# Keeping the relu result and the mean in PSUM in a graph-convolution kernel

## What is computed

```python
def _sage_conv(x, src, dst, W_l, b_l, W_r):
    agg = jax.ops.segment_sum(x[src], dst, num_segments=N_NODES)
    deg = jax.ops.segment_sum(ones(E), dst, num_segments=N_NODES)
    mean = agg / jnp.maximum(deg, 1.0)[:, None]
    return mean @ W_l + b_l + x @ W_r

h = relu(_sage_conv(x, src, dst, W1_l, b1, W1_r))
h = relu(_sage_conv(h, src, dst, W2_l, b2, W2_r))
return _layernorm(x + h @ W3 + b3)
```

## Time and profile before

| what | value |
|---|---|
| timed runs, median of 3 | 2997.61 us (2995.03 to 3005.15) |
| span of the profiled execution | 2989.1 us |
| PE busy | 2869.4 us, 96% |
| DVE busy | 2445.0 us, 82% |
| POOL busy | 2151.1 us, 72% |
| ACT busy | 1997.4 us, 67% |

### The profile page before, as it was taken

One profiled execution on the slowest core, in us unless ns is written; L12 is line 12 of the kernel. 1 busy time (PEld: TensorE's weight loads), 2 busy tenths in 40 slices (PEclk: granted clock), 3 DMA queues, 4 the chain that ended last, 5 costly groups with the idle time before them and its releaser, 6 DMA issues. The chain is left out here.

```text
span 2989.1 us, 55620 instructions
## 1 busy us (share of the span) xinstructions
PE 2869.4 (96%) x18457; PEld 2581.4 (86%) x18457; DVE 2445.0 (82%) x4001; ACT 1997.4 (67%) x2992; POOL 2151.1 (72%) x1732
## 2 busy tenths in 40 slices
PE   5999999999999999999999999999999989999996
PEld 4888989898888889898988888898989879888885
DVE  5787887879787878878787878788787879899896
ACT  3676766767676767667676767676676746555554
POOL 5777777777776767667777767677777747777776
PEclk9999999999999999999999999999999999999998
DMA  4444444444444445444444444444444366666663
GB/s 131 151 152 145 162 150 149 154 142 161 152 155 148 153 143 165 149 148 154 143 159 154 155 147 153 145 164 149 148 154 145 130 205 232 235 223 226 238 221 141
DMA packets 253121, 488.25 MB, mean 163 GB/s; under 512 B 37615, under 2 KB 165206, under 8 KB 253090
## 3 DMA queue, kind: packets, MB, share of 16 engines
q1 hardware_dynamic: 202498, 387.58, 38.6%
q0 software_dynamic: 50176, 99.91, 10.3%
q10 hardware_dynamic: 416, 0.40, 0.0%
HBM read 284.67 MB, written 206.22 MB: 164 GB/s over the span
## 5 line engine op out<-in xcount | busy, mean ns | idle before, releaser
L487 ACT ACTIVATE h_full<-pair,bias 128x512 f32<-128x512 f32 x784 | 531.6, 685 | 681.2 <-PE pair L861 666.4
L649 DVE TENSOR_TENSOR h_lo<-h_full,h_hi 128x1024 fp32r<-128x1024 f32 x392 | 651.7, 1663 | 188.3 <-ACT h_hi L489 188.2
L391 POOL TENSOR_TENSOR xb<-xn,b_row 128x1024 f32<-128x1024 f32 x196 | 471.5, 2405 | 297.7 <-DVE y L671 295.9
L345 POOL DMA_INDIRECT xe<-in_x_dram,e_stage x392 | 500.9, 1278 | 176.9 <-issue 97.7
L872 PE MATMUL pair<-w_hi,h_hi 128*128 128x256 f32 x1960 | 565.4, 288 | 26.6 <-DVE h_lo L649 24.5
L872 PE MATMUL pair<-w_lo,h_hi 128*128 128x256 f32 x1960 | 555.3, 283 | 0.0
L872 PE MATMUL pair<-w_hi,h_lo 128*128 128x256 f32 x1960 | 555.2, 283 | 0.0
L489 ACT CAST h_hi<-h_full 128x1024 fp32r<-128x1024 f32 x392 | 412.0, 1051 | 12.5
L872 PEld LDWEIGHTS pair<-w_hi,h_hi 128*128 128x128 f32 x1960 | 375.6, 192 | 51.7 <-DVE h_lo L649 47.7
L500 ACT ACTIVATE o<-y,nb,rs 128x256 f32<-128x256 f32 x784 | 407.2, 592 | 5.6 <-DVE nb L702 5.3
L861 PE MATMUL pair<-xt_hi,w_hi 128*128 128x512 f32 x980 | 401.6, 410 | 7.9 <-DVE xt_lo L645 4.3
(11 more groups left out here) (124 smaller groups left out, 6439.6 us busy)
## 6 DMA issues: line engine op xcount, KB each, us to landing
xn<-in_x_dram SPq DMA_DIRECT2D x196, 512.0 KB, 4.0
out_dram<-o SPq DMA_DIRECT2D x196, 512.0 KB, 2.6
seg<-seg_tab SPq DMA_DIRECT2D x74, 512.0 KB, 5.1
xdb_tab<-xdb SPq DMA_DIRECT2D x49, 512.0 KB, 4.8
h_tab<-src_h SPq DMA_DIRECT2D x49, 512.0 KB
h_tab<-dst_h SPq DMA_DIRECT2D x49, 512.0 KB, 6.3
xn<-h_tab SPq DMA_DIRECT2D x49, 512.0 KB, 5.1
xb<-xdb_tab SPq DMA_DIRECT2D x49, 512.0 KB, 4.1
```

What stands on the lines that cost most here:

```text
L345: nc.gpsimd.indirect_dma_start(out=xe[:, kind, s], out_offset=None, in_=x, in_offset=bass.IndirectOffsetOnAxis(ap=e_stage[:, kind, s:s + 1 ...
L391: nc.gpsimd.tensor_tensor(xb[:, b], xn[:, u], b3_row[:, :].unsqueeze(1).to_broadcast([P, S, D]), ALU.add).then_inc(xb_ok, 1)
L487: nc.scalar.activation(h_full[:, n, k], ps[:, k], ACT.Relu, bias=bias[:, n, k:k + 1]).then_inc(hf_ok[n], 1)
L649: nc.vector.tensor_tensor(h_lo[:, h], h_full[:, n], h_hi[:, h].bitcast(f32), ALU.subtract).then_inc(hlo_ok[n], 1)
```

## The change

In both phases the relu writes back into the PSUM pair that it reads, and the cast to `h_hi` and the subtraction to `h_lo` read that pair in place of `h_full`. In the edge phase the mean goes into pair[0] in place of the SBUF tile `mean`, after the scans have read the source rows there; its cast and subtraction read pair[0]. A pair is then free only when the subtraction has read it, so three of PE's waits change: `turn_rows` waits for `hlo_ok[0]` in place of `hf_ok[0]`; `turn_edges` of j+1 for `c_mlo_ok` of j in place of the scans of j; `columns` of j for `c_hlo_ok` of j-1 in place of its relus. ACT's and DVE's waits that kept `h_full` and `mean` from being overwritten go. The tile `mean` stays for the edge work in the main loop.

```diff
--- before.py
+++ after.py
@@ -483,10 +483,9 @@
 
                 for k in range(K):
                     act.wait_ge(l_ps[n], g * K + k + 1)
-                    after(act, hlo_ok[n], g)
-                    nc.scalar.activation(h_full[:, n, k], ps[:, k], ACT.Relu, bias=bias[:, n, k:k + 1]).then_inc(hf_ok[n], 1)
+                    nc.scalar.activation(ps[:, k], ps[:, k], ACT.Relu, bias=bias[:, n, k:k + 1]).then_inc(hf_ok[n], 1)
                 act.wait_ge(hf_ok[n], (g + 1) * K)
-                nc.scalar.copy(h_hi[:, h], h_full[:, n]).then_inc(hhi_ok[n], 1)
+                nc.scalar.copy(h_hi[:, h], ps[:, :, :]).then_inc(hhi_ok[n], 1)
 
             def deviation(g, b):
                 act.wait_ge(mv_ok, g + 1)
@@ -546,17 +545,16 @@
 
             def mean_high(j, b):
                 act.wait_ge(c_mean_ok, j + 1)
-                nc.scalar.copy(xt_hi[:, b], mean[:, :, :]).then_inc(c_mhi_ok, 1)
+                nc.scalar.copy(xt_hi[:, b], pair[0][:, :, :]).then_inc(c_mhi_ok, 1)
 
             def second(j, k):
 
-                after(act, c_hlo_ok, j)
                 act.wait_ge(c_l2_ps, j * K + k + 1)
-                nc.scalar.activation(h_full[:, 1, k], pair[2][:, k], ACT.Relu, bias=bias_c[:, k:k + 1]).then_inc(c_hf_ok, 1)
+                nc.scalar.activation(pair[2][:, k], pair[2][:, k], ACT.Relu, bias=bias_c[:, k:k + 1]).then_inc(c_hf_ok, 1)
 
             def second_high(j, b):
                 act.wait_ge(c_hf_ok, (j + 1) * K)
-                nc.scalar.copy(h_hi[:, b], h_full[:, 1]).then_inc(c_hhi_ok, 1)
+                nc.scalar.copy(h_hi[:, b], pair[2][:, :, :]).then_inc(c_hhi_ok, 1)
 
             def deviation_edges(j, b):
                 act.wait_ge(c_mv_ok, j + 1)
@@ -644,9 +642,9 @@
                 dve.wait_ge(xhi_ok, g + 1)
                 nc.vector.tensor_tensor(xt_lo[:, b], ps[:, :, :], xt_hi[:, b].bitcast(f32), ALU.subtract).then_inc(xlo_ok, 1)
 
-            def low_h(g, n, h):
+            def low_h(g, n, h, ps):
                 dve.wait_ge(hhi_ok[n], g + 1)
-                nc.vector.tensor_tensor(h_lo[:, h], h_full[:, n], h_hi[:, h].bitcast(f32), ALU.subtract).then_inc(hlo_ok[n], 1)
+                nc.vector.tensor_tensor(h_lo[:, h], ps[:, :, :], h_hi[:, h].bitcast(f32), ALU.subtract).then_inc(hlo_ok[n], 1)
 
             low_x(0, 0, pair[2])
             nc.vector.tensor_tensor(w_lo[:, X1R + 1:], w_raw[:, X1R + 1:], w_hi[:, X1R + 1:].bitcast(f32), ALU.subtract).then_inc(w_ok, 1)
@@ -657,7 +655,7 @@
             assert done[0] == PREP_RDEG
             dve.wait_ge(cleared, 7)
 
-            low_h(0, 0, 0)
+            low_h(0, 0, 0, pair[0])
             dve.wait_ge(b_in, 96)
             nc.vector.tensor_scalar(b1_row[:, :], b1_row[:, :], -1.0, None, ALU.mult).then_inc(b1_ok, 1)
             nc.vector.tensor_copy(b1_hi[:, :, :], bias[:, 0].unsqueeze(2).to_broadcast([P, K, 2])).then_inc(b1_ok, 1)
@@ -748,14 +746,14 @@
                     if not (first and u < 2):
                         factors_rows(g - 2, u % 2)
                     if not (last and u == 3):
-                        low_h(g + 1, 0, (u + 1) % 2)
+                        low_h(g + 1, 0, (u + 1) % 2, pair[(u + 1) % 4])
                     edges(i, u, pair[(u + 2) % 4])
                     if first and u == 1:
                         dve.wait_ge(seg_out, 64)
                     if not (first and u == 0):
                         residual_rows(g - 1, (u + 1) % 2, pair[(u + 3) % 4])
                         moments_rows(g - 1, (u + 1) % 2)
-                    low_h(g, 1, 2)
+                    low_h(g, 1, 2, pair[u])
                     if last and u == 2:
 
                         dve.wait_ge(slots_ok, NE)
@@ -780,8 +778,7 @@
 
             def means(j, b):
                 dve.wait_ge(c_run_ok, (j + 2) * K)
-                after(dve, c_mhi_ok, j)
-                nc.vector.tensor_tensor(mean[:, :, :], run[:, :, :], seg_of(b)[:, G:2 * G].unsqueeze(1).to_broadcast([P, K, G]), ALU.mult)\
+                nc.vector.tensor_tensor(pair[0][:, :, :], run[:, :, :], seg_of(b)[:, G:2 * G].unsqueeze(1).to_broadcast([P, K, G]), ALU.mult)\
                     .then_inc(c_mean_ok, 1)
 
             def low_dst(j, b):
@@ -791,11 +788,11 @@
 
             def mean_low(j, b):
                 dve.wait_ge(c_mhi_ok, j + 1)
-                nc.vector.tensor_tensor(xt_lo[:, b], mean[:, :, :], xt_hi[:, b].bitcast(f32), ALU.subtract).then_inc(c_mlo_ok, 1)
+                nc.vector.tensor_tensor(xt_lo[:, b], pair[0][:, :, :], xt_hi[:, b].bitcast(f32), ALU.subtract).then_inc(c_mlo_ok, 1)
 
             def low_second(j, b):
                 dve.wait_ge(c_hhi_ok, j + 1)
-                nc.vector.tensor_tensor(h_lo[:, b], h_full[:, 1], h_hi[:, b].bitcast(f32), ALU.subtract).then_inc(c_hlo_ok, 1)
+                nc.vector.tensor_tensor(h_lo[:, b], pair[2][:, :, :], h_hi[:, b].bitcast(f32), ALU.subtract).then_inc(c_hlo_ok, 1)
 
             def residual_edges(j, b):
                 dve.wait_ge(c_xb_in[b], slot_use(j, b))
@@ -956,7 +953,7 @@
                 for u in range(U):
                     g = i * U + u
                     if not (last and u >= 2):
-                        pe.wait_ge(hf_ok[0], (g + 1) * K)
+                        pe.wait_ge(hlo_ok[0], g + 1)
                         turn_rows(i + (u + 2) // U, (u + 2) % U, pair[u])
                     if not (last and u == 3):
                         pe.wait_ge(xlo_ok, g + 2)
@@ -999,7 +996,7 @@
 
             def turn_edges(j, b):
                 pe.wait_ge(c_hs_in[b], slot_use(j, b, 16 * S))
-                pe.wait_ge(c_run_ok, (j + 1) * K)
+                after(pe, c_mlo_ok, j)
                 for k in range(K):
                     turn(pair[0], xn[:, b], k).then_inc(c_hs_ps, 1)
                 pe.wait_ge(c_hd_in[b], slot_use(j, b))
@@ -1017,7 +1014,7 @@
                     pe.wait_ge(y_ok, NG)
                 pe.wait_ge(c_mlo_ok, j + 1)
                 pe.wait_ge(c_hdlo_ok, j + 1)
-                after(pe, c_hf_ok, j * K)
+                after(pe, c_hlo_ok, j)
                 for m in range(K):
                     columns([(X2R, xe_hi[:, b], xe_lo[:, b]), (X2L, xt_hi[:, b], xt_lo[:, b])], pair[2], m).then_inc(c_l2_ps, 1)
                 if not (isinstance(j, int) and j == 0):
```

## The result

| what | before | after |
|---|---|---|
| median of the timed runs (four of each) | 2997.47 us (2995.03 to 3005.15) | 2919.20 us (2916.10 to 2922.27) |
| ratio after : before | | 0.9736, 95% interval 0.9721 to 0.9750 |
| span of the profiled execution | 2989.1 us | 2914.3 us |
| POOL busy in the span | 2151.1 us | 1820.8 us |

The change is faster by 2.6%, 78 us on the medians and 74.8 us between the two profiled spans. Where the 74.8 us come from can be read from first and last starts. The transposes of `xe`, 16 blocks in each of the 49 passes, mark the main loop: here is their line before and after (count, ns min/median/max, first and last start).

What follows compares the result with a forecast made beforehand. PE bounds the main loop, where it waits for h_lo; POOL's DMA issuing bounds the edge phase. Span 2989.1 - 44 (main loop) - 18 (edge phase) = 2927, plus 8.5 between span and median: 2936 us, range 2908 to 2972.

Steps and rivals of the forecast that it cites:

- Forecast A: Whole kernel: main-loop and edge gains both arrive, 2936 us, by itself 2918 to 2955; chance 0.50.
- B: Edge phase: POOL meets `mean` no more, PE bounds at 10.5 us a step; -33 for -18, 2921 us; chance 0.12.
- Low half, main loop: Main loop: subtraction to h_lo falls from 1663 to about 1212 ns, ending PE's two waits a pass; -44 us.
- The bound of -47.7: Main loop: largest gain allowed, PE's weight loads' listed wait for h_lo, 47.7 us in 97 places.
- the far bound: Writing PSUM takes as long again: ACT's relu 1.37 us; DVE's edge `mean` 1.2 us a step more.
- Rival E: Main loop: relu into its own bank is long, deciding from about 1.25 us; slower, 3024 us at 0.685 more; chance 0.06.
- Edge phase: Edge phase: xt_lo and h_lo subtractions stop holding POOL, about 0.7 of 22.38 us a cycle; -18 us, bounds +14 and -33.
- The moved edge waits: Edge phase: transposes' wait bites 0.4 us in one step of two, taken from slack; 10 us if none left.
- C: Edge phase: POOL meets `mean` in every step, two steps cost 22.8 us; +10 instead of -18, 2964 us; chance 0.16.
- The edge bound of -33: Edge phase: largest gain allowed, with PE's 10.5 us a step as floor, (22.38 - 21.0) x 24.
- D: Main loop: gain at u = 1 is lost again, only some 20 us come back; 2960 us; chance 0.11.
- F: Whole kernel: no change, low halves with a PSUM input would still stop for POOL; chance 0.05.

Runs made afterwards that it cites:

- e5: Kernel before, with POOL's adds xb and xdb cut to 8 of 256 columns and all operands left in SBUF: 2948.41 us, ratio 0.9837.
- e3: Kernel before, with only the second layer's h kept in PSUM in the main loop, edge phase as before: 2947.70 us, ratio 0.9848.
- e4: Kernel before, with only the first layer's h kept in PSUM in the main loop, and PE's moved wait: 2995.15 us, ratio 1.0001.
- e8: Changed kernel, with the edge phase's h back in SBUF and its old waits, mean still in PSUM: 2940.14 us, ratio 0.9813.
- e6: Changed kernel, with the edge mean as run times a constant (one source, division by degree left out): 2901.79 us, ratio 0.9689.
- e7: Changed kernel, with the edge phase's mean back in SBUF and its old PE wait, h still in PSUM: 2925.68 us, ratio 0.9769.
- e10: Changed kernel, with the edge scan writing back into PSUM, mean reading it there, and ACT copying the carry to SBUF: 2905.94 us, ratio 0.9673.
- e1: Kernel before, with only the main-loop part of the change, edge phase as before: 2944.72 us, ratio 0.9833.
- e9: Changed kernel, with the edge scan writing back into PSUM, mean reading it there, and DVE copying the carry to SBUF: 2913.76 us, ratio 0.9704.

## Why the prediction was right, and where its sizes were off

Forecast A was 2936 with a range of 2908 to 2972; 2919.2 lies in it and the sign was right. The lower end is wider than its own reason: B with the whole 47.7 gives 2989.1 - 47.7 - 33 + 8.5 = 2917. The sum missed by 16.4 us: 5.4 in the main loop, 8.6 in the edge phase, 3.6 in what was carried around the span, less 1.2 that beginning and passage cost.

*What bounds the kernel: right.* That a DVE operation with two SBUF inputs and a POOL add exclude each other, read from the two ends 1.09 after the adds, is shown by e5, where the adds alone are cut short, by e3 against e4, and by the timeline after.

*Low half, main loop: right, -49.4 where -44 stood.* The subtraction came out at 1216 (forecast 1212) and u = 1 at the forecast margin: it ends at 1002.44, the load starts at 1002.52. The 0.6 us set aside for places that are late was not used. The bound of -47.7 was itself too tight, since it took PE's idle rows for the whole loss. The row of the weight load at u = 0 shows 0.23 idle; the matmuls show what the pass lost. Before (PE, same place as 1001.75 above, at u = 0):

```profile
1011.45 1.04 PE L851 MATMUL pair<-ident,xe 128*128 128x128 f32 x8
1012.48 0.39 PE L872 MATMUL pair<-w_hi,h_hi 128*128 128x256 f32 x1
1012.71 0.28 PE L872 MATMUL pair<-w_lo,h_hi 128*128 128x256 f32 x1
```

From the transposes to the second matmul it was 1.26 there and 1.70 at u = 1 (1021.83 to 1023.53), and it is 1.00 after (1001.75 to 1002.75). That is 0.96 a pass, 47 us in 49 passes, against 0.91 from the idle rows: behind a stall the first matmul also stands longer ahead of the second, 0.23 in place of 0.20 here. The rest, 2.4 of the 49.4 us, I have not placed.

*ACT: the value right, the far bound not needed.* The relu into its own bank takes 660 ns, 25 less than the 685 taken. Rival E, which needed 1.25 us, falls. ScalarE's writes to PSUM being the quicker ones, as the Trainium skill has it (ScalarE: Activation LUTs, section Step-by-step: what each stage is for), agrees with that: 685 to 660 ns. The cast gained 36 ns where 45 stood.

*The moved main-loop wait: right.* It cost nothing (e4).

*Edge phase: the mechanism right, the term too small, -26.6 where -18 stood.* POOL's issues by line, before and after:

```profile
L437 POOL DMA_INDIRECT out_dram<-o,idx x196 | 218.3, 1114 | 62.6 <-issue 58.5 <-ACT o L570 3.8 <-DMA out_dram<-o,idx 0.3
L429 POOL DMA_INDIRECT xn<-h_tab,h_row x196 | 215.0, 1097 | 89.6 <-issue 57.9 <-PE pair L851 21.8 <-DMA h_tab<-dst_h 9.6
```

```profile
L437 POOL DMA_INDIRECT out_dram<-o,idx x196 | 201.6, 1028 | 64.4 <-issue 56.4 <-ACT o L568 5.5 <-PE pair L848 2.1
L429 POOL DMA_INDIRECT xn<-h_tab,h_row x196 | 200.6, 1024 | 92.4 <-issue 55.8 <-PE pair L848 13.2 <-DMA out_dram<-o 12.2
```

The mean issue got 73 and 86 ns shorter, 196 x (0.073 + 0.086) = 31 us in all, of which 26.6 arrived at the end. The sum took away the share of the two subtractions alone: "In the cycle shown they cost it 1.32 - 1.0 and 1.36 - 1.0, about 0.7 us of 22.38", 17 us over 24 cycles (the 18 in the sum has no row for the last 1). That share was sized well: by the table of held issues it is 19.1. What was wrong is the other half of the step, that `mean` would go on costing 1.0 in each cycle. Its share fell from 28.9 to 18.6: 45 issues in place of 53 began inside a `mean`, and later in it. In e8, with `h_lo` back, it is 30.0, so where POOL's issues meet `mean` hangs on what else holds them. Nor is the cycle shown the whole phase: in the kernel before the first thirteen steps have no long one, and after them about every other step is long. How much an issue loses could have been read from the earlier trace rows: the three issues there that stand beside their operation end 0.81 to 0.86 after it.

The mean into PSUM took 1.22, as taken; the far bound of as long again falls. The moved edge waits cost nothing in the running phase (e6, e7), as forecast; the 1.4 us at its start were not foreseen.

*The rivals.* C, POOL meets `mean` in every step: the mechanism is real, `mean` still holds issues (2505.33 above), but not in every step (27 issues lose more than 0.1 us in the 49 steps after), so the cycle came down. B, in which POOL meets `mean` no more, is what e6 is: it gives 10.09 a step, so the floor of 10.5 for PE was too high. That was PE's busy share of a stretch with stalls in it, times the long cycle. The edge bound of -33 was too near accordingly: e6's phase is 41.0 shorter than that of the kernel before (575.0 to 534.0). D, the gain at u = 1 lost again, did not come, since the margin held. F, low halves that still stop for POOL, falls with L647's 1216.

*Around the span: wrong.* The 8.5 us between the span and the median were carried over whole, as if they lay around the span. The profiled run after took 2916.1 with a span of 2914.3: 1.8 lie around it. With the same 1.8 the profiled execution of before took 2990.9, so most of the 8.5 was only that it lay under the median of its kind, and that does not carry over.

## What to carry to other kernels

Where an operation of two inputs on DVE runs beside POOL, leave one input in PSUM if it is there already: the subtraction then takes its 1.2 us whatever POOL does, and POOL's DMA issues keep their 1.0. What such an exclusion costs is counted over all meetings, each put down to the operation that it met, and not taken from one cycle: take one holder away, and the meetings with the others change as well. And a gain of this kind is not complete until the last such operation is gone: look for it in the trace of the new kernel, since here about a third of what the edge phase had to give (14.4 of 41.0 us) was still there.

## What the runs showed of the hardware

POOL's indirect DMA issues, not only its adds, are held by a DVE `tensor_tensor` with two SBUF inputs: 0.94 to 1.03 us alone (e6, e10), up to 2.02 beside one (after). A held issue ends 0.81 to 0.90 us after the operation in which it began (before and after); an issue that was at work before the operation began is not held (1.00 at 2515.20, after). The Trainium skill (SBUF — State Buffer, section Who interferes with whom) takes it, as inferred, that `tensor_tensor` does not stall descriptor generation; here the measurement decides against that for issues whose row list stands in SBUF. Whether the list's reading or the descriptors are held, no run here shows. In the main loop POOL's issues met it too, without a price: the gathers of `xe` went from 1278 to 1036 ns on the mean, and e3, in which they take 1390, has the same pass as e1.

ACT and DVE write the PSUM bank that they read at next to no loss here: relu 660 ns (685 into SBUF), the scan of e9 in place 1275 (1267 into SBUF in the kernel after), `mean` of e9 1222 (1227 in the kernel after, which reads SBUF alone).
